# Values of all groups computed once ahead of the loop and kept in DRAM, the copies of transposed probabilities all issued by SyncE, and a new written-out order, in a one-core attention and gated-FFN kernel

## The reference, cut to what matters

```python
x  = L0_attn_q                               # (1, 1024, 512) f32
xn = layernorm(x)
q, k, v = split(xn @ w_qkv.T)                # 32 query heads, 8 key/value groups, head size 128
scores  = einsum('bskgd,btkd->bkgst', q, k) / sqrt(128)   # causal mask, softmax
attn    = einsum('bkgst,btkd->bskgd', probs, v)
s = attn @ w_dense.T                         # (1024, 4096) @ (4096, 512)
h = relu(s0 * (xn @ sign(k0))) * 2           # two such layers, then k2
g = silu(ffn(xn))
out = x + s * g
```

## Time and profile before

| | |
|---|---|
| median of 3 runs | 915.27 us (912.52 to 916.16) |
| the profiled execution, its time | 917.22 us |
| its span in the trace | 915.1 us |
| busy share: PE, PEld, DVE, ACT, POOL | 98%, 83%, 74%, 56%, 51% |
| granted TensorE clock, mean of the span | 0.997 |
| HBM | 95 GB/s over the span |
| DMA queues q1 (SP), q10 (ScalarE) | 55.9% and 6.9% of 16 engines' time |

### The profile page before, as it was taken

One profiled execution on the slowest core, in us unless ns is written; L12 is line 12 of the kernel. 1 busy time (PEld: TensorE's weight loads), 2 busy tenths in 40 slices (PEclk: granted clock), 3 DMA queues, 4 the chain that ended last, 5 costly groups with the idle time before them and its releaser, 6 DMA issues.

```text
span 915.1 us, 15937 instructions
## 1 busy us (share of the span) xinstructions
PE 896.1 (98%) x4272; PEld 757.4 (83%) x4272; DVE 677.7 (74%) x1163; ACT 513.2 (56%) x1077; POOL 463.3 (51%) x372
## 2 busy tenths in 40 slices
PE   7999999999999999999999999999999999999997
PEld 6878778888788878888788887888788887888886
DVE  7768767787677867788667876788677786678865
ACT  3656645665466645666356644666456663555633
POOL 5246443564346635555336634465445563355775
PEclk9999999999999999999999999999999999999999
DMA  6496655857386764865577573867549664655472
GB/s 218 121 249 192 132 115 156 241 132 152 66 239 197 155 120 115 244 165 118 103 192 222 136 155 61 243 185 153 109 127 255 157 124 86 171 151 125 103 202 86
DMA packets 204806, 143.58 MB, mean 157 GB/s; under 512 B 23152, under 2 KB 172144, under 8 KB 204784
## 3 DMA queue, kind: packets, MB, share of 16 engines
q1 hardware_dynamic: 176112, 129.68, 55.9%
q10 hardware_dynamic: 28672, 13.64, 6.9%
...
## 4 chain that ended last, share of the span: by engine, by line
issue 51%; POOL 30%; PE 14%; DMA 2%; SPq 1%; DVE 1%; POOLq 1%; ACT 0%; DVEq 0%
POOL pt_lo L767 21%; POOL w_lo L777 6%; POOL wd_lo L777 3%; PE ps_m L1251 3%; PE ps_s L1236 2%; PE ps_o L1119 1%; PE ps_o L1121 1%; PE ps_o L1120 1%; PE ps_m L1119 1%; PE ps_m L1120 1%; PE ps_m L1121 1%; PE ps_s L1120 1%; PE ps_s L1121 1%; PE ps_s L1119 1%; SPq L674 1%
## 5 line engine op out<-in xcount | busy, mean ns | idle before, releaser
L767 POOL TENSOR_TENSOR pt_lo<-pt_lo,pt_hi 128x512 fp32r<-128x512 f32 x248 | 326.2, 1339 | 257.6 <-ACT pt_hi L866 257.6
L959 DVE CUSTOM_DVE_ANT_0 ps_s<-ps_s,mask 128x32 f32<-128x32 f32 (+31 forms) x256 | 181.8, 716 | 93.7 <-PE ps_s L1121 92.2
L866 ACT ACTIVATE pt_hi<-pt_lo 128x512 fp32r<-128x512 f32 x288 | 172.6, 628 | 78.7 <-PE ps_o L1121 42.8
L1119 PE MATMUL ps_m<-xn_hi,w_hi 128*128 128x512 f32 (+1 forms) x388 | 152.2, 392 | 1.8 <-DVE q_lo L1067 1.8
L1121 PE MATMUL ps_m<-xn_hi,w_lo 128*128 128x512 f32 (+1 forms) x388 | 150.9, 389 | 0.0
L1120 PE MATMUL ps_m<-xn_lo,w_hi 128*128 128x512 f32 (+1 forms) x388 | 150.8, 389 | 0.0
L819 ACT ACTIVATE prob_even<-ps_s,small 128x32 f32<-128x32 f32 (+15 forms) x128 | 82.8, 648 | 99.5 <-DVE small L959 98.1
L819 ACT ACTIVATE prob_odd<-ps_s,small 128x160 f32<-128x160 f32 (+15 forms) x128 | 96.1, 754 | 63.1 <-DVE small L959 36.4
L1120 PE MATMUL ps_s<-k_lo,q_hi 128*128 128x480 f32 (+15 forms) x384 | 126.6, 330 | 0.0
L1121 PE MATMUL ps_s<-k_hi,q_lo 128*128 128x480 f32 (+15 forms) x384 | 126.5, 329 | 0.0
L1119 PE MATMUL ps_s<-k_hi,q_hi 128*128 128x480 f32 (+15 forms) x384 | 124.7, 325 | 0.0
...
## 6 DMA issues: line engine op xcount, KB each, us to landing
...
```

Of the source, the lines that this page charges most:

```text
L767: pool.tensor_tensor(pt_lo[:, slot, :], pt_lo[:, slot, :].bitcast(F32), pt_hi[:, hi_slot, :], ALU.subtract).then_inc(land_lo, 1)
L866: act.activation(pt_hi[:, hi_slot, :], pt_lo[:, LAND_AT[i] + j, :].bitcast(F32), ACT.Copy).then_inc(land_hi, 1)
L959: dve.tensor_tensor_reduce(out=scores, in0=scores, in1=mask[:, S - width(i % BLOCKS, tile):S], scale=-1.0, scalar=BIG, op0=ALU.add, op1=AL ...
L1119: pe.matmul(out, sta_hi, mov_hi, start=start, stop=False)
```

## The change

The values of all eight groups are computed in the prologue: for each half of the groups (four groups, 512 columns of weights) and each row block, twelve matmuls with `xn` stationary and the weights moving (`values.half.b`), which leaves keys on the partitions. DVE copies each result to one of four stages in `prob_even`, SP stores it in a DRAM tensor `values` (`store`), and each round loads its group's half as 128x512 into `v_lo` (`vload`), which ScalarE and POOL split. The `v` piece and `vblocks` are gone from the rounds, with the first unit's computation in two halves of 256 columns. Layernorm goes in pairs of blocks instead of fours. `RAW` is 3 instead of 5, `LAND` 16 instead of 12, and `LAND_AT`, `LAND_AFTER` are new. ScalarE issues no DMA any more: `move` issues four for each b. Row blocks 0 to 3 go through DRAM as before. All tables are new; of them two lines are shown.

```diff
--- before.py
+++ after.py
-RAW = 5
+RAW = 3
 HI_RING = 4
-LAND = 12
+LAND = 16
...
-ACT_HEADS = (3,)
-
-PIECES = ["q0", "q1", "q2", "q3", "k", "v"]
+PIECES = ["q0", "q1", "q2", "q3", "k"]
...
-LAND_AT = [0, 1, 3, 6, 1, 6, 0, 4]
+LAND_AT = [0, 6, 12, 8, 1, 10, 1, 8]
 COLUMNS = [list(range(i + 1)) for i in range(BLOCKS)]
 COLUMNS[6].reverse()
 
-LAND_AFTER = {0: tri(7), 2: 30 - PAIRS, 3: 34 - PAIRS, 4: tri(3), 5: tri(4), 6: tri(5) + 1, 7: tri(6) + 3}
+LAND_AFTER = {0: tri(1), 1: 23 - PAIRS, 2: 35 - PAIRS, 3: 32 - PAIRS, 4: tri(7) - PAIRS, 5: tri(4), 6: tri(5),
+              7: tri(6)}
...
+    pe = ln(0, 1) + values(0, 0, 1) + ln(2, 3) + values(0, 2, 3) + unit("q0") + ln(4, 5) + unit("q1") \
+        + ln(6, 7) + unit("q2") + unit("q3") + unit("k") + values(0, 4, 5, 6, 7) \
+        + [("scores", first, r) for r in tiles] + values(1, *blocks)
...
+    dve = stats[0] + moments[:1] + scale[0] + lo(*ln(0, 1)) + stats[1] + moments[1:2] + scale[1] \
+        + lo(*values(0, 0), *ln(2, 3), *values(0, 1)) + stats[2] + moments[2:3] + lo(*values(0, 2)) + scale[2] \
+        + lo(*values(0, 3), *ln(4, 5), q0) + stats[3] + moments[3:] + scale[3] \
+        + lo(*ln(6, 7), q1, q2, q3, k, *values(0, 4, 5, 6, 7))
+    dve += [("max", first, r) for r in tiles] + lo(*values(1, 0)) + [("flip", first), ("inverse", first)] \
...
+    sp = x[0:2] + wv_load[0] + x[2:4] + load[0:2] + x[4:6] + load[2:3] + x[6:8] + wv_load[1] \
+        + store[0][0:2] + load[3:4] + store[0][2:4] + load[4:5] + store[0][4:] \
+        + [("scales",), ("vload", 0), ("dw", first), ("rw", first)] + store[1][0:2] \
+        + [("dr", first), ("rr", first)] + store[1][2:]
...
 BODY = {
     "pe": """
...
-        scores.4.1 vblocks.1 weigh.1.0 dense.0.0 scores.4.2 dense.0.1 scores.4.3 dense.0.2
...
+        weigh.5.4 weigh.5.5 unit.k.0.0 unit.k.0.1 unit.k.0.2 unit.k.0.3 unit.q3.0.0 unit.q3.0.1
...
+                    elif what == "store":
+                        half, b = item
+                        sp.wait_ge(shared_read, r.shared_no(("values", half, b)))
+                        groups = slice(half * HALF_GROUPS, (half + 1) * HALF_GROUPS)
+                        sp.dma_start(values_d[groups, :, b, :].rearrange("g t d -> t g d"),
+                                     stage(half, b).rearrange("t (g d) -> t g d", d=P))\
+                          .then_inc(values_stored[value_no(half, b) % STAGES], 16)
+                    elif what == "vload":
+                        half, = item
+
+                        ahead = 1 - half
+                        for stored_part in values_stored:
+                            sp.wait_ge(stored_part, 16 * BLOCKS // STAGES * (1 if kind == "prologue" else 2))
+                        if kind != "prologue":
+                            sp.wait_ge(block_weighed, WEIGHED0 + PAIRS * g + (PAIRS - HALF // P) * ahead)
+                        keys = slice(half * HALF // P, (half + 1) * HALF // P)
+                        src = values_d[bass.ds(g + ahead, 1), :, keys, :].rearrange("a t b d -> (a t) b d")
+                        sp.dma_start(v_lo[:, keys, :].bitcast(F32), src).then_inc(values_loaded[half], 16)
...
+                            if i == BY_DRAM:
+                                sp.sem_inc(flips_seen)
+                                sp.wait_ge(land_hi, r.pair(i - 2, COLUMNS[i - 2][0]))
                         slots = slice(LAND_AT[i], LAND_AT[i] + i + 1)
-                        for h in range(HEADS - len(ACT_HEADS)):
+                        for h in range(HEADS):
...
-                    if what == "amove":
-                        i, b = item
-                        act.wait_ge(flipped, r.flip_no(i, b))
-                        if b == 0:
-                            act.wait_ge(block_weighed, WEIGHED0 + PAIRS * g + LAND_AFTER[i])
-                        slots = slice(LAND_AT[i], LAND_AT[i] + i + 1)
-                        for h in ACT_HEADS:
-                            act.dma_start(pt_lo[b * Q:(b + 1) * Q, slots, h * P:(h + 1) * P].bitcast(F32),
-                                          prob_quadrants(i)[h * Q:(h + 1) * Q, :, b, :])\
-                               .then_inc(landed[i % 2], 16)
-                        continue
                     if what == "silu":
...
+                    elif name == "values":
+                        _, half, b = item
+                        dve.wait_ge(shared_done, r.shared_no(item))
+                        n = value_no(half, b)
+                        if n >= STAGES:
+                            dve.wait_ge(values_stored[n % STAGES], 16 * (n // STAGES))
...
-                    elif name == "vblocks":
-                        half = item[1]
-
-                        pe.wait_ge(shared_read, max(r.order.index(item) - 2,
-                                                    r.order.index(("unit", "v", half))) + 1 + r.shared0)
-                        for n in range(4):
-                            mm = pe.transpose(bank[:, n * P:(n + 1) * P], vt[:, n * P:(n + 1) * P],
-                                              ident[:, :])
+                    elif name == "values":
+                        _, half, b = item
+                        no = r.shared_no(item)
+                        if no > 2:
+                            pe.wait_ge(shared_read, no - 2)
+                        pe.wait_ge(ln_lo, b + 1)
+                        for c in range(CHUNKS):
+                            if b == 0:
+                                pe.wait_ge(wv_split, wv_no(half, c) + 1)
```

More of the change, by code:

```diff
@@ L125, in has_hi @@
 def has_hi(item):
-    return item[0] in ("vblocks", "hidden") or (item[0] == "unit" and item[1] != "v")
+    return item[0] in ("unit", "hidden")
 def parse(tokens):
@@ L145, in prologue @@
     ln = lambda *blocks: [("ln", b) for b in blocks]
-    values = [("vblocks", 0)]
-    tiles = range(TILES)
-    first = BLOCKS
-    pe = ln(0, 1, 2, 3) + unit("q0") + unit("q1") + unit("q2") + ln(4, 5) + unit("q3") + ln(6, 7) \
-        + unit("k") + unit("v") + [("scores", first, r) for r in tiles] + values
-    units = [("unit", p, 0) for p in ("q0", "q1", "q2", "q3", "k", "v")]
+    values = lambda half, *blocks: [("values", half, b) for b in blocks]
     hi = lambda *items: [("hi", item) for item in items]
@@ L164, in prologue @@
-    dve += [("max", first, r) for r in tiles] + [("flip", first), ("inverse", first)] + lo(*values)
-    pool = lo(*split) + [("zero_odd",)]
-    sp = [("load", p) for p in PIECES + [f"wd{h}" for h in range(HEADS)]] + [("scales",), ("dw", first), ("rw", first), ("dr", first), ("rr", first)]
+    tiles = range(TILES)
+    blocks = range(BLOCKS)
+    first = BLOCKS
+    pe = ln(0, 1) + values(0, 0, 1) + ln(2, 3) + values(0, 2, 3) + unit("q0") + ln(4, 5) + unit("q1") \
+        + ln(6, 7) + unit("q2") + unit("q3") + unit("k") + values(0, 4, 5, 6, 7) \
+        + [("scores", first, r) for r in tiles] + values(1, *blocks)
@@ new lines, in prologue @@
+    q0, q1, q2, q3, k = [("unit", p, 0) for p in PIECES]
+    wv = [[("wv", half, c) for c in range(CHUNKS)] for half in range(2)]
+    split = [("split", p) for p in PIECES]
+    root = [("root", n) for n in range(BATCHES)]
+    act = hi(wv[0][0]) + root[:1] + hi(*wv[0][1:], *ln(0, 1)) + root[1:2] + hi(split[0], *ln(2, 3), split[1]) \
+        + root[2:3] + hi(split[2], *ln(4, 5), q0, split[3]) + root[3:] \
+        + hi(*ln(6, 7), q1, split[4], q2, *wv[1][:2], q3, *wv[1][2:], k)
+    act += [("exp", first, r) for r in tiles] + hi(("vload", 0))
@@ L329, in shared @@
     return [whole(i) for i in ORDERS[kind]["pe"]
-            if i[0] == "vblocks" or (i[0] in ("unit", "dense", "hidden") and i[-1] == CHUNKS - 1)]
+            if i[0] == "values" or (i[0] in ("unit", "dense", "hidden") and i[-1] == CHUNKS - 1)]
 PRO_SHARED, BODY_SHARED = len(shared("prologue")), len(shared("body"))
@@ L922, in moments @@
             def moments(half):
[L924 removed]
+                blocks = slice(half * 2, half * 2 + 2)
                 base = LN_STEPS * half
```

430 lines of the change are left out of this document (227 added, 203 removed).

## The result

The changed kernel took 922.49, 923.78 and 926.52 us, against 912.52 to 916.16 (median 915.12) of the kernel before: ratio 1.0104, 95% interval 1.0066 to 1.0142, so it is slower by about 1%. (A fourth run took 4589.27 us; the records don't show why, it is left out of the ratio, and none of the six later runs of the same kernel did it.) Those six, 926.25 to 931.94 us, gave 1.0120 (1.0099 to 1.0142). Forecast were 909 us and 899 to 919; the time lies outside, on the other side.

A forecast was written before the change was run, and what follows sets the result against it. A round was taken as bound by TensorE's issue time plus 2.1 us. Terms -7.3 - 0.2 + 3.5 + 0 - 2.0 + 0 summed to -6.0 us, giving 909 us on the median of 915.27, range 899 to 919.

The forecast's parts named there:

- A ring of three ... row blocks 1 to 3 behind it have 7 us or more between landing and weighing: 0: SP's queue in rounds: weight loads wait for splits three pieces earlier, but row blocks 1 to 3 have slack; 0 us.
- Its list is 129.2 ... SP's 16 DMAs of row block 7 have 25.8 us of cover: 0: Last group: TensorE's list of 129.2 us, less 3.2 for values counted elsewhere; row block 7's DMAs are covered; 0 us.
- Prologue +3.5: Prologue: a 2.4 us TensorE gap before blocks 6, 7 and about 1 before the second values pair; between -1 and +6.
- rival (913): Prologue gives most of the gain back: the clock falls at the gap and locks hit each moments; +4, 913, chance 0.20.
- First round -2.0: First round: values computed before the loop give late engines time, removing its 2.1 us over a later round; -2.0 us.
- Row 7: wait 0.1 to 2.2: Each round, before row block 7's first weighing: TensorE waits 0.1 to 2.2 us, where it waited 1.0 before.
- SP's four extra DMAs: Rounds, row blocks 4 to 7: 16 issues instead of 12, paid by an earlier start; unpaid, +2.6 us a round.
- The rival on SP's queue: Rounds: SP's queue becomes the bound for row blocks 5 to 7; a round 2 us longer gives 923, chance 0.15.
- Transposes -7.3, all of it on TensorE, so it counts in full: Sixteen groups of value transposes, 0.46 us each, leave TensorE's list and shorten the total by 7.3 us.

The follow-up runs named there:

- e6: Changed kernel with two items of unit q2 ahead of row block 3's first weighing on TensorE in each round; ratio 1.0066 to the kernel before.
- e13: Changed kernel with the loads of q3 and k, and their splits, moved behind row block 4's copies and last slot; ratio 1.0051 to the kernel before.
- e5: Changed kernel; in the last group the load of k0 stands behind wd3's and ScalarE splits wd0 ahead of exp.2.0; ratio 1.0061 to the kernel before.
- e3: Changed kernel with head 3's copies of row blocks 4 to 7 issued by ScalarE again; ratio 1.0119 to the kernel before.
- e4: Kernel before with only one of the four transposes of each vblocks kept; ratio 0.9968 to the kernel before.
- e8: e7 plus 52 warm-up matmuls, row block 7's seventh-slot lo on DVE, and the last group's build.1 behind lo of hidden.0.0.3; ratio 0.9942 to the kernel before.
- e9: e8 with the last group's build.1 put back ahead of the lo of hidden.0.0.0; 907.37 us, ratio 0.9895 to the kernel before.
- e7: Changed kernel with prologue statistics of blocks 6, 7 earlier, the edits of e5 and e6, and dr.2 ahead of load.q3; 912.15 us, ratio 0.9960 to the kernel before.
- e15: e9 with the loads of q3 and k moved as in e13; 906.07 us, ratio 0.9892 to the kernel before.

## Why the prediction was wrong, by its own steps

Against the forecast (loop entered at 79.0, seven rounds of 99.6, last group 127.9) the profiled execution lost 1.5 us in the prologue, 6.1 in the rounds and 4.3 in the last group.

*"A ring of three ... row blocks 1 to 3 behind it have 7 us or more between landing and weighing: 0"* failed first. From the issue of row 3's read (211.78) TensorE leaves 11.0 us; 6.3 for the old read, 0.6 for `pt_hi`, 1.3 for POOL and about 0.4 between them leave 2.4, not 7, and with a read of 9.3 us it is 0.6 too late. The old list left 13.7, or 7.4 behind a landing of 6.3: the 7 us hold for the list that was replaced. The term was 0 and measured 5.3 us; e6 (two items later) and e13 (fewer bytes ahead) each took 4 to 6 us off at this place. It varies from profile to profile, as the loop entry does; which of them spreads this kernel's runs is not shown.

*"Its list is 129.2 ... SP's 16 DMAs of row block 7 have 25.8 us of cover: 0"*, the last group, failed second, by 4.3 us (132.2 against 127.9). The cover of row 7 was there. But the group's early part now loads all four `wd` pieces that before had come a group earlier, through a ring that blocks SP; e5 took 4.5 us off by moving a load and a split.

*"Prologue +3.5"* was right in its places: locks in the moments (1.27 and 1.28 us at 8.18, 16.89 and 24.49, 0.16 at 34.88), a gap of 2.64 (2.4 forecast), 1.0 before the second pair (1). Its size was too small: the entry was 80.3 to 84.0 in eight profiles instead of 79.0, so the term was 4.8 to 8.5, in six of the eight above its stated bound of 6 (which itself was 1 short: 3.5 and three locks of 1.2 are 7.1). What it left out is the clock, which fell behind the gap in seven of the eight and behind the first wait in seven of the eight, at 1.7 us a stretch; I had kept that as a rival (913), at a chance of 0.20. POOL's subtraction had begun at 8.15, 16.86 and 24.47, 0.03 us or less ahead of the three slow instructions, and none ran at 34.88. The Trainium skill's page "SBUF — State Buffer", section "Who interferes with whom", on the lock of the shared port, agrees with those four rows.

*"First round -2.0"* held: 101.5 and 100.7 us, 1.2 more and 0.1 less than the other six rounds on the mean. Before it was 3.0 more and not 2.1, since the stretch in the earlier trace rows ends at 143.30 and the round at 144.13.

*"Row 7: wait 0.1 to 2.2"* and *"SP's four extra DMAs"* were right: waits of 0 to 0.8 before its first weighing, none before row 6 (0.7 forecast), 0.66 us an issue where 0.65 had been assumed without a row, and by e3 nothing to be had from ScalarE's queue. The rival on SP's queue was wrong as written (e3): SP was not the bound; what it moves ahead of row 3 was.

*"Transposes -7.3, all of it on TensorE, so it counts in full"*: the list is shorter by 7.3, but in the old order only about half comes through (e4), since the splits of row 7 set the pace where one of each two groups of transposes stood. The new list gives 3.1 us back at the same place, until that slot's split moves to DVE (e8, e9).

So sign and size came from taking "no wait there before" for "slack there now": I priced TensorE's list and rows 6 and 7, and put zeros where the list itself had been written anew. With the three places mended (e7) the kernel gains 3.7 us, less than the 6 forecast; with the split of row 7's seventh slot on DVE and the longer warm-up as well 9.6 (e9), and 9.9 (e15), of which 7.3 are the transposes and the rest less waiting (excess over the list 15.7 us in e9_best, 19.6 before). These two edits came together, so their shares are read from profiles alone: from e7 to e9 the entry falls from 78.4 to 76.4 and the mean round from 99.8 to 99.2. What stays open is how much each of the other DMAs around row 3's read adds (7.1 us in e13 against 6.3 before), and some 3 us of the rounds' excess, which lie in steps too small to name.
